# A graph layer on one core: completion signals of TensorE in the second gather stage, from drains to the matmuls themselves

## The chip, the cores and the metric

The kernel runs on one core of a Trainium2 chip. The metric is the device time of one execution in microseconds, the median over several runs. A core has five engines that run side by side and wait for one another by semaphores: TensorE (PE; its weight loads are listed as PEld), VectorE (DVE), ScalarE (ACT), GpSimd (POOL) and SyncE (SP). GpSimd, SyncE and ScalarE also issue DMA transfers here.

## The reference

The input is a graph with 6,250 nodes of 128 features and 100,000 edges, sorted by their destination. Two layers follow one another, each with a residual and a layer norm:

1. a relational layer: the messages `x[src] * norm` are summed by destination and edge type, multiplied by one matrix for each type (a mixture of 8 basis matrices), and a self-loop, a bias and a ReLU follow;
2. an edge layer: for every edge `e = (x[dst] - x[src]) @ theta.T + x[src] @ phi.T`, a batch norm over all edges, a ReLU, a product with `fc1`, a second batch norm and ReLU; the result is averaged over the edges of each destination, and a ReLU follows.

The stage of this document computes the first `e` of the second layer, for all edges. `theta` and `phi` act on nodes, so the kernel has two node tables in DRAM: `btab` (what an edge takes from its source) and `atab` (what it takes from its destination; as three bf16 parts that add up to the f32 value). An edge's `e` is a row of one plus a row of the other. The stage also counts the edges of every node, and the statistics of the batch norm.

## The kernel before, in words

Edges are handled in tiles of 128, chunks of 4 tiles (512 edges) and groups of 4 chunks. There are 49 groups and 196 chunks, the last one partly filled (782 tiles hold edges). The first gather stage (L682, to about 1250 us) belongs to the relational layer, the second one, the edge stage (about 1350 to 2515 us), to the edge layer. After it come a pass over the stored `e` (to 2700 us), the pass that sums by destination (to 3050 us) and the nodes.

In the edge stage each engine has its own program, written out by hand, with loops over pairs of groups. For every chunk:

- **GpSimd** takes one `g_free` and issues four indirect DMAs (L697), one a tile: each brings the 128 rows of `btab` that the sources name into a tile of `G`. `G` has room for two groups, so eight chunks.
- **SyncE** takes one `aw_free` and loads the 80 rows of `atab` from the chunk's least destination on (L618) into one of four buffers `aw`. Once a group it loads the digits of the destinations (L599).
- **TensorE** (`edge_features`) waits for the gathers and for a free bank of PSUM (`e_free`, four banks), and turns the four tiles into the bank (L906, f32). It waits for `aw` and for `ohT_ready`, and adds the destination's row by three matmuls against a one-hot matrix (L911, the "lookup"). It waits for `cnt_oh` and adds four small products to the node counts in bank 7 (L918). Then it spreads the digits of the chunk after next over all partitions (`spread_dst`, L895), into bank 0 or 1. At the end stands a drain (L938), which ends when TensorE has nothing left in work, and which increments `look_done`; `cnt_done` (L939) and `d_ready` (L941) are incremented by the sequencer after it.
- **VectorE** is one chunk ahead: it takes `d_ready` and compares the spread digits with the row numbers, which gives `ohT` (L1477); it takes `cnt_done` and makes the two one-hot factors of the counts (L1466, L1467, two buffers); it takes `e_copied` of an earlier chunk and measures its moments (L1504).
- **ScalarE** takes `look_done`, increments `g_free` (L1099) and `aw_free` (L1100), copies the bank to SBUF (L1101), and increments `e_free` and `e_copied`. Once a group it stores 1 MB of `e` to DRAM (L1107).

All waits go through the helper `take` (L56), so L56 stands in the rows wherever an engine waited for a semaphore. Chunks whose destinations reach beyond 80 nodes would need further windows; there is a second copy of the loop for them (`wide_chunks`), which these inputs don't use: all 196 drains of the trace are those of L938.

In the first gather stage the same four gathers a chunk (L682) fill `G`. TensorE multiplies each tile (L780), and the last of a chunk's four products increments the semaphore that ScalarE's copy (L1046) waits for; the copy's sequencer also gives `g_free` (L1042). A second product (L791) follows from the copy. There is no drain on TensorE in that stage. An f32 product stands as two matmuls in the trace.

Of the kernel before, what the change touches and what calls it, by code (L numbers as in the profile page):

```python
# [52 lines left out]
def take(eng, sem, n=1):  # L53

    eng.wait_ge(sem, n)
    eng.sem_inc(sem, -n)  # L56
# [17 lines left out]
def gnn_kernel(nc, x, src, dst, etype, norm, weight, w_comp, loop_w, h_bias,  # L74
# [38 lines left out]
    def sem(name):  # L113
        return ctx.enter_context(nc.semaphore(name))

    with ctx:  # L116
# [193 lines left out]
        cnt_done = sem("cnt_done")  # L310
# [26 lines left out]
        d_ready = sem("d_ready")  # L337
        ohT_ready = sem("ohT_ready")
        look_done = sem("look_done")
        look_first = sem("look_first")  # L340
# [37 lines left out]
        def reached(eng, name, s, value):  # L378

            eng.wait_ge(s, value)  # L380
            eng.sem_inc(ticks[name], 1)

        def by_pairs(eng, n, body, head=1, tail=0):

            for i in range(2 * head):
                body(i, i % 2, i // 2)
            with eng.Fori(head, n // 2 - tail) as i:
                body(2 * i, 0, i)
                body(2 * i + 1, 1, i)
            for i in range(n - 1 - 2 * tail, n):  # L390
                body(i, i % 2, i // 2)
# [32 lines left out]
        def gathered(g, k, use):  # L424

            return 16 * (TPC * use + len(real_tiles(g, k)))
# [38 lines left out]
        def last(i, n):  # L465
            return isinstance(i, int) and i == n - 1

        def after(g, h, use, k):

            if k + 1 < CPG:  # L470
                return g, h, use, k + 1
            if last(g, NG):
                return None
            return g + 1, 1 - h, use + h, 0

        def widest_chunk(eng):

            return eng.value_load(widest_c[0:1, 0:1], min_val=0, max_val=NXW)

        def reach_of(eng, c):  # L480

            return eng.value_load(bounds[0:1, bass.ds(c, 1)], min_val=SPAN, max_val=SPAN * (NXW + 1) - 1)
# [17 lines left out]
        def by_width(eng, w, loop):  # L500

            with eng.If(w >= 1):
                loop(True)
            with eng.If(w < 1):
                loop(False)
# [12 lines left out]
        def further_windows(eng, reach, body):  # L518

            with eng.If(reach >= 2 * SPAN):  # L520
                with eng.Fori(1, reach // SPAN) as i:
                    body(i)
# [203 lines left out]
        def _(pe):  # L726
# [24 lines left out]
            for k, a in enumerate((theta_s, phi_s, fc1_s)):  # L751
                mm = pe.transpose(PS[:, 6, k * D:(k + 1) * D], a[:, :], ident[:, :])
# [139 lines left out]
            def spread_dst(g, h, use, k):  # L892
                if k == 0:
                    reached(pe, "pe", dig_in[h], 16 * (use + 1))
                pe.matmul(PS[:, k % 2, :], onesb[0:2, :], digits[:, h, k * CHUNK:(k + 1) * CHUNK],  # L895
                          start=True, stop=True)

            def edge_features(wide_chunks):
                def one(g, h, use):
                    for k in range(CPG):  # L900
                        if wide_chunks:
                            reach = reach_of(pe, CPG * g + k)
                        reached(pe, "pe", b_gathered[CPG * h + k], gathered(g, k, use))
                        take(pe, e_free)
                        for q in range(TPC):
                            pe.matmul(PS[:, 2 + k, q * TILE:(q + 1) * TILE], G[:, h, TPC * k + q, :], ident[:, :],  # L906
                                      start=(q == 0), stop=False, is_transpose=True, skip_group_check=True)
                        reached(pe, "pe", aw_in[k], 16 * (g + 1))
                        take(pe, ohT_ready)
                        for a in range(3):  # L910
                            mm = pe.matmul(PS[:, 2 + k, :], aw[0:WIN, k, a, :], ohT[0:WIN, k % 2, :],  # L911
                                           start=False, stop=(a == 2), skip_group_check=True)
                        if wide_chunks:
                            mm.then_inc(look_first, 1)

                        take(pe, cnt_oh)
                        for q in range(TPC):
                            mm = pe.matmul(PS[:, 7, 0:NW], oh_lo[:, k % 2, q, :], oh_hi[:, k % 2, q, :],  # L918
                                           start=(isinstance(g, int) and g == 0 and k == 0 and q == 0),
                                           stop=(last(g, NG) and k == CPG - 1 and q == TPC - 1), skip_group_check=True)  # L920

                        def further(i):
                            take(pe, awx_in, 16)
                            take(pe, ohTx_ready)
                            for a in range(3):
                                mm = pe.matmul(PS[:, 2 + k, :], awx[0:WIN, a, :], ohTx[0:WIN, :],
                                               start=False, stop=(a == 2), skip_group_check=True)
                            mm.then_inc(lookx_done, 1)
                        if wide_chunks:
                            further_windows(pe, reach, further)  # L930
                        nxt = after(g, h, use, k)
                        nxt = nxt and after(*nxt)
                        if nxt:
                            spread_dst(*nxt)
                        if wide_chunks:
                            pe.drain().then_inc(cnt_done, 1)
                        else:
                            pe.drain().then_inc(look_done, 1)  # L938
                            pe.sem_inc(cnt_done, 1)  # L939
                        if nxt:  # L940
                            pe.sem_inc(d_ready, 1)  # L941
                by_pairs(pe, NG, one)
            pe.wait_ge(widest_c_known, 1)
            for k in range(2):
                spread_dst(0, 0, 0, k)
            pe.drain().then_inc(d_ready, 2)
            by_width(pe, widest_chunk(pe), edge_features)


# [772 lines left out]
```

## Time and profile before

| | |
|---|---|
| time, median of 3 runs | 3090.55 us (3073.56 to 3092.17) |
| the profiled execution | 3090.62 us, span 3088.8 us |
| TensorE (PE) busy | 1948.1 us (63%) |
| VectorE (DVE) busy | 1365.8 us (44%) |
| ScalarE (ACT) busy | 614.7 us (20%) |
| GpSimd (POOL) busy | 1605.7 us (52%) |
| mean granted clock of TensorE | 0.712 |

The span is from the first to the last instruction of one profiled execution. Busy time counts an engine's own work, not its waits. The ends of matmuls are modelled, their starts are not. An entry such as `[2.61 <-POOLq L56]` says that the engine was idle for 2.61 us before the instruction, and that a wait at L56 on its own queue ended that time; `issue` stands where the profile shows nothing that was waited for, or only the engine's own pace.

### The profile page before, as it was taken

Reading aid. Unit: us, or ns where it says so; the run is one execution under the profiler, and the core shown is the slowest. Engines: PE = TensorE matmul, PEld = TensorE weight load, DVE = VectorE, ACT = ScalarE, POOL = GpSimd, SP = SyncE. Lnnn points to the kernel's source line nnn. Section 1 sums busy time; section 2 is a strip of 40 time slices with the busy share of each in tenths; the row PEclk is TensorE's granted clock in tenths of the full one; section 3 lists DMA queues with packets and bytes.
Section 4 is the critical chain, followed back from the end, with each engine's and each line's share of the span. In section 5 each row is a group of like instructions: output and inputs, shape, how many; then the busy total and the mean of one; then the engine's idle time right before and its main releaser. Section 6 shows DMA issues by size and latency. Waiting matters only on the chain. (4 is left out here: it accounts for less than half of the span.)

```text
span 3088.8 us, 42986 instructions
## 1 busy us (share of the span) xinstructions
PE 1948.1 (63%) x10210; PEld 1494.5 (48%) x10211; DVE 1365.8 (44%) x3584; ACT 614.7 (20%) x1004; POOL 1605.7 (52%) x1759
## 2 busy tenths in 40 slices
PE   2666566656666666635554545445555579999997
PEld 2555465645655556622222222222222234499996
DVE  4333333333433333533333333333333358877776
ACT  2111111111111111411010101010101137534434
POOL 5665665666666664246666666666666620092002
PEclk9778777778778787855555555555555569999999
DMA  3221212121222211223333333333333349534443
GB/s 87 54 55 53 59 51 56 52 60 54 59 59 53 59 54 40 90 86 95 103 99 94 96 95 93 95 108 96 95 94 96 108 178 308 185 121 143 145 149 96
DMA packets 124080, 291.20 MB, mean 94 GB/s; under 512 B 34957, under 2 KB 77506, under 8 KB 106224
## 3 DMA queue, kind: packets, MB, share of 16 engines
q1 hardware_dynamic: 65856, 136.12, 13.5%
q0 software_dynamic: 50048, 102.50, 12.8%
q10 hardware_dynamic: 8112, 51.91, 4.3%
q14 instruction: 47, 0.39, 0.0%
q8 instruction: 17, 0.28, 0.0%
HBM read 227.22 MB, written 63.18 MB: 94 GB/s over the span
## 5 line engine op out<-in xcount | busy, mean ns | idle before, releaser
L697 POOL DMA_INDIRECT G<-btab,srcT x782 | 737.5, 943 | 534.9 <-POOLq L56 278.6
L682 POOL DMA_INDIRECT G<-in_x,srcT x782 | 746.3, 954 | 469.1 <-issue 233.3
L906 PE MATMUL PS<-ident,G 128*128 128x128 f32 x784 | 212.9, 427 | 568.9 <-PEq L56 335.9
L906 PEld LDWEIGHTS PS<-ident,G 128*128 128x128 f32 x784 | 140.1, 217 | 662.5 <-issue 662.5
L791 PE MATMUL PS<-BIG 128*128 128x192 f32 (+1 forms) x1584 | 352.0, 372 | 126.4 <-issue 124.6
L780 PE MATMUL PS<-BIG,G 128*128 128x192 f32 x1564 | 362.9, 393 | 91.2 <-issue 57.6
L791 PEld LDWEIGHTS PS<-BIG 128*128 128x128 f32 x1584 | 312.8, 222 | 152.9 <-issue 152.6
L1477 DVE TENSOR_SCALAR ohT<-PS,node_col 80x512 bf16<-80x512 f32 x196 | 146.2, 746 | 536.6 <-DVEq L56 317.2
L780 PEld LDWEIGHTS PS<-BIG,G 128*128 128x128 f32 x1564 | 328.6, 237 | 105.3 <-issue 104.8
L1046 ACT ACTIVATE BIG<-PS 128x768 f32<-128x768 f32 x196 | 156.3, 809 | 1032.7 <-ACTq L56 887.4
L1313 DVE SCALAR_TENSOR_TENSOR BIG<-PS,dst0T,BIG 128x192 f32<-128x192 f32 x784 | 324.2, 416 | 79.9 <-issue 67.1
L1322 DVE TENSOR_TENSOR ACC<-ACC,PS 128x24 f32 x782 | 135.3, 173 | 447.3 <-DVEq L56 324.1
L1101 ACT ACTIVATE BIG<-PS 128x512 f32<-128x512 f32 x196 | 117.0, 597 | 1057.0 <-ACTq L56 1029.4
L911 PE MATMUL PS<-ohT,BIG 80*128 80x512 bf16 x588 | 291.4, 633 | 1.9 <-PEq L56 1.9
L978 PE MATMUL PS<-fc1sT,G 128*128 128x128 f32 x1568 | 216.3, 282 | 2.9 <-DVEq L1598 1.5
L1504 DVE BATCH_NORM_STATS2 stats<-BIG 128x6 f32<-128x512 f32 x192 | 131.2, 684 | 181.4 <-issue 112.2
L992 PE MATMUL PS<-BIG 128*128 128x80 f32 x1568 | 198.9, 270 | 0.0
L978 PEld LDWEIGHTS PS<-fc1sT,G 128*128 128x128 f32 x1568 | 192.3, 193 | 3.4 <-DVEq L1598 1.8
L992 PEld LDWEIGHTS PS<-BIG 128*128 128x128 f32 x1568 | 190.6, 192 | 0.0
L1145 ACT ACTIVATE G<-BIG,small 128x512 f32<-128x512 f32 x188 | 137.8, 803 | 207.9 <-ACTq L56 207.9
L958 PE MATMUL PS<-G,fc1T 128*128 128x512 f32 x392 | 170.1, 597 | 6.2 <-PEq L56 6.2
L722 POOL TENSOR_SCALAR X<-X,ln_st,ln_r 128x128 f32<-128x128 f32 x20 | 15.7, 795 | 262.9 <-DVEq L1682 262.9
(182 smaller groups left out, 1834.3 us busy)
## 6 DMA issues: line engine op xcount, KB each, us to landing
BIG<-spill SPq DMA_DIRECT2D x90, 1024.0 KB, 4.9
spill<-BIG ACTq DMA_DIRECT2D x49, 1024.0 KB
G<-in_x,srcT POOLq DMA_INDIRECT x782
G<-btab,srcT POOLq DMA_INDIRECT x782
typ_i<-in_edge_type SPq DMA_DIRECT2D x97, 128.0 KB
BIG<-atab SPq DMA_DIRECT2D x196, 60.0 KB
atab<-BIG SPq DMA_DIRECT2D x12, 384.0 KB
xn<-in_x SPq DMA_DIRECT2D x48, 64.0 KB
```

The lines of the kernel that those rows point to most:

```text
L682: nc.gpsimd.indirect_dma_start(out=G[0:n, g % 2, t, :], out_offset=None, in_=x, in_offset=bass.IndirectOffsetOnAxis(ap=srcT[0:n, TPG * g + ...
L697: nc.gpsimd.indirect_dma_start(out=G[0:n, g % 2, t, :], out_offset=None, in_=btab[:, :], in_offset=bass.IndirectOffsetOnAxis(ap=srcT[0:n, ...
L780: mm = pe.matmul(PS[:, 2 * c + q // 2, (q % 2) * ZW:(q % 2 + 1) * ZW], G[:, h, TPC * k + q, :], soh[:, p, TPC * c + q, :, :].rearrange("p ...
L791: mm = pe.matmul(PS[:, bank, tiles.start * TWIN:tiles.stop * TWIN], basis[:, b, :], zs[:, p, tiles, b, :], start=(b == 0), stop=(b == B - ...
L906: pe.matmul(PS[:, 2 + k, q * TILE:(q + 1) * TILE], G[:, h, TPC * k + q, :], ident[:, :], start=(q == 0), stop=False, is_transpose=True, sk ...
L911: mm = pe.matmul(PS[:, 2 + k, :], aw[0:WIN, k, a, :], ohT[0:WIN, k % 2, :], start=False, stop=(a == 2), skip_group_check=True)
L958: pe.matmul(PS[:, CPG * h + k, :], fc1T[:, :], hot[:, h, k * CHUNK:(k + 1) * CHUNK], start=True, stop=True).then_inc(e2_ready, 1)
L978: mm = pe.matmul(PS[:, k, q * D:(q + 1) * D], hot[:, h, t * TILE:(t + 1) * TILE], fc1sT[:, :], start=True, stop=True)
L992: mm = pe.matmul(PS[:, 4 + k, 0:WIN], R2[:, k, q, :], oh3[:, k, q, :], start=(q == 0), stop=(q == TPC - 1))
L1046: act.activation(zs[:, p, TPC * c:TPC * c + 2 * banks, :, :].rearrange("p (a q) k n -> p a (q k n)", a=banks), PS[:, 2 * c:2 * c + banks, ...
L1313: ins = dve.scalar_tensor_tensor(out=soh[:, p, j, :, :], in0=over(steps0, B, TWIN), scalar=dst0T[:, bass.ds(t, 1)], in1=each(coefs[:, bass ...
L1477: dve.tensor_scalar(ohT[0:WIN, k % 2, :], PS[0:WIN, k % 2, :], node_col[0:WIN, 0:1], None, ALU.is_equal).then_inc(ohT_ready, 1)
```

## The change

In the edge stage TensorE's drains are taken out, and three matmuls signal in their place: the last lookup of a chunk increments `look_done` (the copy of the loop for wide chunks already had a signal there, `look_first`), the last count product increments `cnt_done`, and each spread of digits increments `d_ready`. The same goes for the two spreads and the drain ahead of the loop. The number of increments of each semaphore stays.

```diff
@@ spread_dst
                 pe.matmul(PS[:, k % 2, :], onesb[0:2, :], digits[:, h, k * CHUNK:(k + 1) * CHUNK],
-                          start=True, stop=True)
+                          start=True, stop=True).then_inc(d_ready, 1)
@@ edge_features
                         for a in range(3):
                             mm = pe.matmul(PS[:, 2 + k, :], aw[0:WIN, k, a, :], ohT[0:WIN, k % 2, :],
                                            start=False, stop=(a == 2), skip_group_check=True)
-                        if wide_chunks:
-                            mm.then_inc(look_first, 1)
+                        mm.then_inc(look_first if wide_chunks else look_done, 1)
 
                         take(pe, cnt_oh)
                         for q in range(TPC):
                             mm = pe.matmul(PS[:, 7, 0:NW], oh_lo[:, k % 2, q, :], oh_hi[:, k % 2, q, :],
...
+                        mm.then_inc(cnt_done, 1)
...
                         if nxt:
                             spread_dst(*nxt)
-                        if wide_chunks:
-                            pe.drain().then_inc(cnt_done, 1)
-                        else:
-                            pe.drain().then_inc(look_done, 1)
-                            pe.sem_inc(cnt_done, 1)
-                        if nxt:
-                            pe.sem_inc(d_ready, 1)
                 by_pairs(pe, NG, one)
             pe.wait_ge(widest_c_known, 1)
             for k in range(2):
                 spread_dst(0, 0, 0, k)
-            pe.drain().then_inc(d_ready, 2)
             by_width(pe, widest_chunk(pe), edge_features)
```

## Rows read from the trace of the kernel before

**Rows 1.** Busy times of the edge stage: stretch, engines, PEclk, DMA share, GB/s

```profile
1350.00:2515.00 1165.00, 598.86 (x2344) 319.29 (x2345) 445.40 (x827) 116.43 (x195) 712.97 (x751) 0.50 0.31 96
```

**Rows 2.** Groups of instructions, 1400 to 2490 us: busy us, mean ns, idle before

```profile
L906 PE MATMUL PS<-ident,G 128*128 128x128 f32 x720 | 195.6, 427 | 539.4 <-PEq L56 313.4 <-issue 226.0
L1477 DVE TENSOR_SCALAR ohT<-PS,node_col 80x512 bf16<-80x512 f32 x180 | 134.3, 746 | 508.8 <-DVEq L56 297.8 <-issue 206.9 <-PEq L941 4.1
L1466 DVE TENSOR_TENSOR oh_lo<-PS,loT 128x512 bf16<-128x512 f32 x179 | 121.1, 677 | 0.0
L1467 DVE TENSOR_TENSOR oh_hi<-PS,hiT 128x196 bf16<-128x196 f32 x179 | 62.3, 348 | 0.0
L1504 DVE BATCH_NORM_STATS2 stats<-BIG 128x6 f32<-128x512 f32 x180 | 123.1, 684 | 168.4 <-issue 110.0 <-DVEq L56 58.4
```

**Rows 3.** GpSimd's gathers, 1400 to 2490 us: durations; waits (total us, times, longest)

```profile
L697 POOL DMA_INDIRECT G<-btab,srcT x720: 867/944/955, 1400.2 to 2489.7; - x180
POOL G L697 <- POOLq L56: 172.7, 54, 4.0
POOL G L697 <- ACTq L1099: 26.6, 18, 2.0
```

**Rows 4.** The drain's line: duration ns min/median/max, first and last start

```profile
L938 PEldq DRAIN  x196: 1965/3914/10583, 1353.6 to 2514.6; - x196
```

**Rows 5.** Timeline of TensorE in the edge stage: start us, us, instruction [idle before]

```profile
2005.91 1.09 PE L906 MATMUL PS<-ident,G 128*128 128x128 f32 x4 [4.12 <-PEq L56]
...
2008.38 0.60 PE L895 MATMUL PS<-BIG,onesb 2*128 2x512 bf16 x1
2009.66 1.09 PE L906 MATMUL PS<-ident,G 128*128 128x128 f32 x4 [0.68 <-issue]
2010.54 1.49 PE L911 MATMUL PS<-ohT,BIG 80*128 80x512 bf16 x3
...
2012.13 0.60 PE L895 MATMUL PS<-BIG,onesb 2*128 2x512 bf16 x1
2018.34 1.08 PE L906 MATMUL PS<-ident,G 128*128 128x128 f32 x4 [5.61 <-PEq L56]
```

**Rows 6.** Timeline of ScalarE in the same stretch

```profile
2009.26 0.60 ACT L1101 ACTIVATE BIG<-PS 128x512 f32<-128x512 f32 x1 [3.15 <-ACTq L56]
2017.94 0.60 ACT L1101 ACTIVATE BIG<-PS 128x512 f32<-128x512 f32 x1 [8.09 <-ACTq L56]
```

**Rows 7.** Timeline of GpSimd in the same stretch

```profile
2006.17 0.94 POOL L697 DMA_INDIRECT G<-btab,srcT  x1 [2.50 <-POOLq L56]
...
2015.05 0.94 POOL L697 DMA_INDIRECT G<-btab,srcT  x1 [0.30 <-issue]
2018.60 0.94 POOL L697 DMA_INDIRECT G<-btab,srcT  x1 [2.61 <-POOLq L56]
```

**Rows 8.** GpSimd's gathers in the first stage, 60 to 1250 us, as rows 3

```profile
L682 POOL DMA_INDIRECT G<-in_x,srcT x750: 875/944/1470, 68.7 to 1217.3; - x188
POOL G L682 <- ACTq L1042: 127.9, 41, 4.2
POOL G L682 <- POOLq L56: 98.7, 45, 15.4
```

**Rows 9.** Timeline of TensorE and ScalarE in the first gather stage

```profile
703.74 2.77 PE L780 MATMUL PS<-BIG,G 128*128 128x192 f32 x16
708.85 0.32 PE L791 MATMUL PS<-BIG 128*128 128x192 f32 x1 [2.34 <-issue]
...
713.50 1.51 ACT L1046 ACTIVATE BIG<-PS 128x768 f32<-128x768 f32 x2 [11.35 <-ACTq L56]
```

**Rows 10.** Timeline of TensorE after the last gather

```profile
2507.27 1.09 PE L906 MATMUL PS<-ident,G 128*128 128x128 f32 x4 [0.68 <-PEq L56]
...
2511.03 1.09 PE L906 MATMUL PS<-ident,G 128*128 128x128 f32 x4 [0.68 <-PEq L56]
```

## The prediction

> **What bounds the kernel now.** I began with the page and its chain of waits. The chain holds only the last few instructions, so it says nothing of the stage that is changed; I went to that stage by its lines. The edge stage runs from about 1350 to 2515 us. The busy times of that stretch [rows 1] show no engine full: GpSimd 713 of 1165 us, TensorE 599, at a granted clock of 0.50 (the 1.2 GHz level).
>
> What could bound it is read from the groups. GpSimd issues four gathers a chunk, 943 ns each with a usual gap of 0.30 us between them [rows 3, 7], so a chunk costs it 4 * 1.25 = 5.0 us. VectorE's four large instructions a chunk add up to 0.746 + 0.677 + 0.348 + 0.684 = 2.46 us [rows 2]. TensorE's chunk lasts 3.07 us from the first transpose (2009.66) to the end of the spread (2012.13 + 0.60) [rows 5]. So GpSimd should set the pace, yet the 180 chunks between 1400 and 2490 us took 1090 / 180 = 6.06 us each.
>
> The waits tell why. In that stretch GpSimd stood 172.7 + 26.6 = 199.3 us in 72 waits for a free chunk of G [rows 3]. Without the wait each would have been the usual 0.30 us gap, so the waits cost 199.3 - 72 * 0.30 = **178 us**, 2.47 us apiece, one in every 180 / 72 = 2.5 chunks. This is the ceiling of what the change can give in the stage. The free chunk is signalled by ScalarE (L1099) once it has look_done, and look_done comes from TensorE's drain.
>
> The drain's own row [rows 4] has a median of 3.9 us and a longest of 10.6 us. It starts while matmuls are still queued, so its length alone isn't the loss; the timeline [rows 5, 6] is. The chunk from 2005.91 ends with a spread at 2008.38 + 0.60 = 2008.98, and ScalarE starts 0.28 us later. The next chunk's spread ends at 2012.73, but ScalarE starts at 2017.94, 5.2 us later, and TensorE's next transpose at 2018.34, after 5.61 us idle. Nothing that the profile names was running on TensorE. In that time GpSimd had issued its eighth gather (2015.05, ended 2015.99), then waited 2.61 us for the chunk that this very drain had to free [rows 7]. So the picture of a cycle is: GpSimd resumes (2006.17), TensorE's first chunk passes at once (+2.8 us), the second, which ends at +6.6 us, is held until gathers have stopped, GpSimd runs dry, the signal comes, and it begins again: two chunks in 12.43 us.
>
> **Is it the drain, or TensorE's signals as such?** The first gather stage has the same gathers and no drain. There a run of L780 starts at 703.74 and lasts 2.77 us: two chunk products of equal length, so the first one's own signal (it stands on its last matmul) was due near 705.1 (an estimate, half of the run). ScalarE's copy that waits for it starts at 713.50, after 11.35 us idle, and TensorE itself issues L791 singly, with 2.34 us idle before the first one [rows 9]. So while gathers flow, a matmul's own signal is held as well, and so is the issue of further matmuls. This is the main evidence against the change.
>
> A page speaks to the same point: the Trainium skill, Perfetto Trace Analysis, section "Tensor Engine Instruction (MATMUL, LD_WEIGHTS)", says that the end shown for a matmul is an estimate and that its semaphore goes out only when PSUM has acknowledged the write. By that rule the matmuls would end late, not the drain, and the change would give almost nothing; the trace of the first stage agrees in the 8.4 us between 705.1 and 713.50.
>
> **The change part by part.** *Removed:* 196 drains, 196 increments of cnt_done and 194 of d_ready on TensorE's sequencer. Where nothing holds the drain, a chunk step has 0.68 us between the last matmul and the next transpose [rows 5, 10]; inside a chunk TensorE's groups follow without idle time. Without the drain this gap goes, hidden under GpSimd's 5.0 us a chunk, except after the last gather (2489.7 [rows 3]): the seven chunks that then remain run at 2511.03 - 2507.27 = 3.76 us each, and become 3.07. That is 7 * 0.68 = 5 us, on the path to the end of the stage. If VectorE became the bound there (2.46 us of work), nothing changes.
>
> *Added:* three signals a chunk on matmuls that are there already. No row has their price alone. From below: the runs of L780 with two signals inside them show no gap [rows 9], so 0. From above: the 0.68 us gap of the three sequencer steps that they replace. I take 0, the nearer row. Even the upper end would lie under TensorE's idle time, 539.4 / 180 = 3.0 us a chunk [rows 2]; with that cover gone it would be 0.68 * 196 = 133 us, which the range doesn't hold, since the gap goes with the steps.
>
> A second rule of the skill speaks against the change: TensorE: Matmul & The Clock Gate, section "The cost: per-tile semaphore tail", gives 26.3 ns for each matmul that signals, one after another. By it the sum would be worse by an estimated 3 * 26.3 ns * 196 = 15 us if they stood on the path; no run here shows it.
>
> *Moved:* look_done goes from behind the spread to the last lookup, 0.70 us earlier in the chunk (2010.54 + 1.49 = 2012.03 against 2012.73). The lost gap brings the second chunk forward by another 0.68 us, so its look_done falls at +5.2 us after GpSimd resumes instead of +6.6. ScalarE then gives g_free, aw_free and its copy earlier. SP's window loads and the digits are four chunks and a group ahead, and SP and ScalarE's queues issue the same DMAs in the same order; nobody waits for them. cnt_done and d_ready stay in order on VectorE: it takes d_ready of the chunk after next first, and it is one chunk ahead.
>
> *What is late next:* the drain also kept TensorE from the following chunk. Its transposes need a free bank (four deep), its lookups an ohT that VectorE made from the spread two chunks back. So when chunk B's signals are held, TensorE can still do all of chunk C; chunk D's lookups need B's spread signal. At the next quiet moment B and C are signalled together, if B was not signalled in time already.
>
> **The sum.** A cycle today frees on the strict pattern one held chunk and one that passes (2), and 2.5 on average. After the change it frees one or two held ones and two that pass (3 to 4). I take 3.5. Waits: 180 / 3.5 = 51 instead of 72, at 2.47 us: 127 us instead of 178, a gain of 51, and 5 at the tail: 56 us. At 3 chunks: 60 waits, 148 us, gain 35; at 4: 45 waits, 111 us, gain 72. The profiled execution took 3090.62 us (span 3088.8 and 1.8 around it), the median is 3090.55, so the sum holds for both: 3090.6 - 56 = **3035 us**, 3019 to 3056 for this case alone. It stays in the sum that the waits keep their length.
>
> **The rivals.**
> *No change (chance 0.27).* The signals on matmuls are held just as long and only the tail is won: 3085 us. For it: the first stage [rows 9], whose 86 waits cost 226.6 - 86 * 0.30 = 201 us in 187.5 chunks [rows 8], 1.07 us a chunk against 0.99 here, without any drain. If the edge stage took over exactly that price it would be 196 * 0.08 = 16 us worse, 3101 with the tail. Against it: in the held chunk all matmuls still started without a gap, so what is held is what comes last, and look_done no longer comes last.
> *GpSimd becomes the bound (0.08).* All 178 us and the tail go: 2908 us. TensorE's 3.07 us and VectorE's 2.46 would allow it; against it speaks that the hold is seen in both gather stages whenever several gathers are in flight. A higher granted clock in a denser stage would push this way.
> *Slower (0.10).* TensorE, not stopped any more, sends a third chunk into the gather flow; its instructions wait singly as L791's do, and the signals of the held chunks stand behind them. The number of waits stays at 72, but each lasts longer. The first stage's waits for ScalarE have a mean of 127.9 / 41 = 3.1 us, the longest here is 4.0 [rows 3, 8]. At 3.5 us: 72 * 3.2 = 230 us, 52 worse, less 5: 3138 us; at 4.0 us 3174. It decides from a wait of 3.3 us on (72 * 3.0 = 216, +38 - 5).
> *That the change doesn't do what it says* can be left out as a case of its own: the plain branch is the one that runs, with 196 drains in it [rows 4].
>
> **The numbers.** Forecast 0.55, no change 0.27, GpSimd's bound 0.08, slower 0.10. Faster by over 1% means below 3060 us; a measurement of this kernel can hardly tell less than 1% from no change. Faster: nearly all of 0.55, and 0.08, less what the forecast may fall short: 0.58. Slower by over 1% (above 3121): 0.10. The same: 0.32. The range leaves out GpSimd's bound and the slower case: from 2985 (six chunks a cycle: 30 waits, 74 us, gain 104 and the tail 5, gives 2982) to 3100 (the first stage's price).
>
> **What would show it.** Right: no drain in the edge stage, the step of the last seven chunks near 3.1 us, ScalarE's copy starting within 0.3 us of the second chunk's lookups after a resume, and GpSimd's waits near 50 with a mean under 3 us. Wrong: about 70 waits again, with copies 5 us behind their lookups (no change); waits above 3.3 us with single matmuls among long gaps in the edge stage (slower); gathers 1.25 us apart throughout (GpSimd's bound).

## The result, and the profile after

The changed kernel took 3044.34 us (median of 4 runs, 3042.78 to 3047.93), the kernel before 3091.36 us beside it: a ratio of **0.987** (95% interval 0.984 to 0.990). The forecast was 3035 us, range 2985 to 3100. The time is right, but one term of the sum is not.

Line numbers shift by up to eight: L1469 was L1477, L1093 was L1101 (the copy), L917 was L918; there is no drain. The profiled execution took 3043.06 us, against 3090.62. Three moments of either trace split the 47.6 us; two of them, the first and the last gather, stand in these rows (before, then after):

```profile
L697 POOL DMA_INDIRECT G<-btab,srcT x782: 867/944/958, 1288.1 to 2489.7; - x196
L697 POOL DMA_INDIRECT G<-btab,srcT x782: 869/944/961, 1278.9 to 2448.5; - x196
```

| part of the profiled execution | before | after | difference |
|---|---|---|---|
| start to the first gather of the edge stage | 1288.1 | 1278.9 | -9.2 |
| first to last gather (start to start) | 1201.6 | 1169.6 | -32.0 |
| last gather to the end of ScalarE's last copy | 27.8 | 20.7 | -7.1 |
| from there to the end | 573.1 | 573.9 | +0.8 |

The first line isn't the change's: nothing before the edge stage was edited, and over the twelve kernels below that moment lies anywhere from 1275.7 to 1296.7 us. What the change gave is in the second and third lines, 39 us in these two executions; the interval of the ratio puts it between 30 and 48 us.

The busy times of the stage after, to be set beside [rows 1]:

```profile
1350.00:2470.00 1120.00, 604.28 (x2315) 290.03 (x2315) 431.35 (x819) 115.84 (x194) 708.90 (x747) 0.50 0.32 100
```

GpSimd fills 709 of 1120 us, still not full; the granted clock is 0.50 as before. Its gathers and waits from 1400 us on, and the groups, answering to [rows 2, 3]:

```profile
L697 POOL DMA_INDIRECT G<-btab,srcT x712: 869/944/961, 1399.3 to 2448.5; - x178
POOL G L697 <- issue: 202.6, 651, 1.7
POOL G L697 <- POOLq L56: 176.3, 61, 4.3
```

```profile
L911 PE MATMUL PS<-ohT,BIG 80*128 80x512 bf16 x534 | 257.8, 620 | 486.5 <-issue 168.7 <-DVE ohT L1469 138.3 <-PEq L56 131.1
L906 PE MATMUL PS<-ident,G 128*128 128x128 f32 x716 | 199.5, 434 | 0.0
L1469 DVE TENSOR_SCALAR ohT<-PS,node_col 80x512 bf16<-80x512 f32 x178 | 132.2, 743 | 614.5 <-DVEq L56 382.4 <-remote 190.0 <-issue 40.7
L1093 ACT ACTIVATE BIG<-PS 128x512 f32<-128x512 f32 x178 | 106.3, 597 | 939.2 <-ACTq L56 846.3 <-issue 54.1 <-DVEq L1521 38.8
```

The lookups before, from 1400 to 2490 us, had no idle time ahead of them:

```profile
L911 PE MATMUL PS<-ohT,BIG 80*128 80x512 bf16 x540 | 267.6, 633 | 0.0
```

TensorE's idle time has moved from the transposes (539.4 us ahead of L906 before, 0.0 now) to the lookups (486.5 us ahead of L911): it now runs on into the next chunk and stands at the next `ohT`, whose spread is not signalled yet. The lists put some stops of GpSimd under "issue" and some 0.3 us gaps under a wait, so from here on a **stop** is a distance of over 1.5 us between the starts of two gathers, where 1.25 is usual, and its cost is what exceeds 1.25. From 1400 us to the last gather there were 82 stops of 2.34 us (191.6 us) before, and 48 of 3.37 us (161.8 us) after. One cycle after, as a timeline:

```profile
1781.27 0.60 ACT L1093 ACTIVATE BIG<-PS 128x512 f32<-128x512 f32 x1 [15.66 <-ACTq L56]
1781.93 0.94 POOL L697 DMA_INDIRECT G<-btab,srcT  x1 [3.85 <-POOLq L56]
...
1782.34 0.60 ACT L1093 ACTIVATE BIG<-PS 128x512 f32<-128x512 f32 x1 [0.47 <-ACTq L56]
...
1784.21 0.60 ACT L1093 ACTIVATE BIG<-PS 128x512 f32<-128x512 f32 x1 [1.28 <-DVEq L1521]
...
1784.22 1.11 PE L906 MATMUL PS<-ident,G 128*128 128x128 f32 x4
...
1785.19 1.44 PE L911 MATMUL PS<-ohT,BIG 80*128 80x512 bf16 x3
...
1786.89 0.60 ACT L1093 ACTIVATE BIG<-PS 128x512 f32<-128x512 f32 x1 [2.08 <-ACTq L56]
...
1787.54 18.07 SPq L618 DMA_DIRECT2D BIG<-atab  x4
...
1789.29 1.44 PE L911 MATMUL PS<-ohT,BIG 80*128 80x512 bf16 x3 [0.91 <-DMA BIG<-atab]
...
1795.01 1.44 PE L911 MATMUL PS<-ohT,BIG 80*128 80x512 bf16 x3 [2.54 <-DVE ohT L1469]
...
1800.66 0.94 POOL L697 DMA_INDIRECT G<-btab,srcT  x1 [0.31 <-issue]
...
1804.75 0.60 ACT L1093 ACTIVATE BIG<-PS 128x512 f32<-128x512 f32 x1 [17.27 <-ACTq L56]
...
1805.42 0.94 POOL L697 DMA_INDIRECT G<-btab,srcT  x1 [3.81 <-POOLq L56]
1805.64 1.44 PE L911 MATMUL PS<-ohT,BIG 80*128 80x512 bf16 x3 [7.44 <-PEq L56]
1805.82 0.60 ACT L1093 ACTIVATE BIG<-PS 128x512 f32<-128x512 f32 x1 [0.47 <-ACTq L56]
```

Four copies a cycle: two held chunks come out together (0.47 us apart), and two more pass. GpSimd then issues 16 gathers (1781.93 to 1800.66) and stops for 3.81 us beyond its last gather, where [rows 7] show 2.61 us after eight. The lookups that start at 1789.29 and 1795.01 have their copies only at 1804.75 and 1805.82: the first signal is 14.0 us late, where the one of [rows 6] was 5.2. It is the signal that is late and not ScalarE: the trace records no change of the semaphore `look_done` between 1786.64 and 1804.51 us, and ScalarE's wait ends at 1804.53. The tail, answering to [rows 10]:

```profile
2454.50 1.11 PE L906 MATMUL PS<-ident,G 128*128 128x128 f32 x4
...
2457.53 1.11 PE L906 MATMUL PS<-ident,G 128*128 128x128 f32 x4
...
2460.55 1.11 PE L906 MATMUL PS<-ident,G 128*128 128x128 f32 x4
```

After the last gather a chunk takes 3.03 us instead of 3.76.

### The profile page after: what moved, and what is told of

Read it like the earlier page. It is cut to its first block and busy times, and to the rows that moved or that the text cites. A ratio compares the mean times of both kernels' runs of the same rounds, so it can differ in the third digit from the quotient of the medians.

```text
span 3041.2 us, 42399 instructions
## 1 busy us (share of the span) xinstructions
PE 1975.9 (65%) x10210; PEld 1477.7 (49%) x10211; DVE 1357.8 (45%) x3584; ACT 614.1 (20%) x1004; POOL 1606.5 (53%) x1759
## 5 line engine op out<-in xcount | busy, mean ns | idle before, releaser
L911 PE MATMUL PS<-ohT,BIG 80*128 80x512 bf16 x588 | 284.3, 621 | 516.9 <-issue 168.7
L791 PE MATMUL PS<-BIG 128*128 128x192 f32 (+1 forms) x1584 | 369.6, 382 | 142.5 <-issue 140.6
L1469 DVE TENSOR_SCALAR ohT<-PS,node_col 80x512 bf16<-80x512 f32 x196 | 145.5, 742 | 649.6 <-DVEq L56 413.1
L791 PEld LDWEIGHTS PS<-BIG 128*128 128x128 f32 x1584 | 323.9, 229 | 180.7 <-issue 180.4
L911 PEld LDWEIGHTS PS<-ohT,BIG 80*128 80x128 bf16 x588 | 64.0, 127 | 626.4 <-issue 623.2
L1093 ACT ACTIVATE BIG<-PS 128x512 f32<-128x512 f32 x196 | 117.0, 597 | 1019.7 <-ACTq L56 915.3
L906 PE MATMUL PS<-ident,G 128*128 128x128 f32 x784 | 218.4, 434 | 4.2 <-PEq L56 4.2
L984 PEld LDWEIGHTS PS<-BIG 128*128 128x128 f32 x1568 | 190.6, 192 | 0.0
L906 PEld LDWEIGHTS PS<-ident,G 128*128 128x128 f32 x784 | 140.0, 216 | 89.8 <-issue 89.8
```

Of the source, the lines that this page charges most:

```text
L791: mm = pe.matmul(PS[:, bank, tiles.start * TWIN:tiles.stop * TWIN], basis[:, b, :], zs[:, p, tiles, b, :], start=(b == 0), stop=(b == B - ...
L984: mm = pe.matmul(PS[:, 4 + k, 0:WIN], R2[:, k, q, :], oh3[:, k, q, :], start=(q == 0), stop=(q == TPC - 1))
L1469: dve.tensor_scalar(ohT[0:WIN, k % 2, :], PS[0:WIN, k % 2, :], node_col[0:WIN, 0:1], None, ALU.is_equal).then_inc(ohT_ready, 1)
```

## The experiments

All twelve in one table: the ratio of times to the kernel before, first to last gather, the one long stop before the first copy (start to start), and the stops from 1400 us on.

| kernel | ratio [95%] | first to last gather | first stop | stops | their cost | mean | cost per gather |
|---|---|---|---|---|---|---|---|
| before | 1 | 1201.6 | 29.7 | 82 | 191.6 | 2.34 | 0.27 |
| after | 0.987 [0.984, 0.990] | 1169.6 | 27.1 | 48 | 161.8 | 3.37 | 0.23 |
| e1 bare drain | 1.003 [1.001, 1.005] | 1199.3 | 28.1 | 66 | 191.1 | 2.90 | 0.27 |
| e2 look_done last | 0.992 [0.990, 0.994] | 1175.8 | 28.8 | 54 | 166.8 | 3.09 | 0.23 |
| e3 g_free early | 0.987 [0.983, 0.990] | 1160.2 | 23.7 | 53 | 154.2 | 2.91 | 0.22 |
| e4 light TensorE | 0.985 [0.982, 0.988] | 1154.0 | 26.1 | 43 | 151.5 | 3.52 | 0.21 |
| e5 small windows | 0.989 [0.987, 0.991] | 1180.5 | 28.9 | 51 | 171.2 | 3.36 | 0.24 |
| e6 small stores | 0.988 [0.986, 0.991] | 1177.7 | 29.3 | 45 | 166.2 | 3.69 | 0.23 |
| e7 all small | 0.983 [0.982, 0.985] | 1170.8 | 28.1 | 48 | 160.5 | 3.34 | 0.23 |
| e8 four ahead | 0.986 [0.984, 0.988] | 1179.4 | 28.5 | 46 | 168.0 | 3.65 | 0.23 |
| e9 half the rows | 0.987 [0.983, 0.992] | 1172.4 | 30.0 | 57 | 193.4 | 3.39 | 0.27 |
| e10 half the bytes | 0.989 [0.985, 0.993] | 1167.5 | 27.9 | 47 | 162.2 | 3.45 | 0.23 |
| e11 long pause | 1.013 [1.007, 1.018] | 1259.5 | none | 187 | 259.4 | 1.39 | 0.36 |
| e12 short pause | **0.974** [0.971, 0.978] | 1137.4 | none | 185 | 146.5 | 0.79 | 0.21 |

(e9's gathers are shorter, 0.91 us, so its stops count against 1.21 us. In e11 and e12 each pause counts as a stop.)

**e1: a drain that signals nothing.** At the end of each chunk, with the matmuls' own signals kept:

```diff
                         if nxt:
                             spread_dst(*nxt)
+                        pe.drain()
```

> The changed kernel with the drain back at the end of each chunk, but without a signal: look_done, cnt_done and d_ready stay on the matmuls. Theory A (while gathers flow, everything that TensorE finishes is held back in order, and a wait of GpSimd ends when gathers have stopped and TensorE's backlog is worked off): TensorE can't run a chunk ahead in the hold, so a wait frees one held chunk and two that pass, 3 instead of 4, and each wait is short again, about 2.5 us over the usual gap as in the kernel before instead of about 3.5: some 62 waits, 155 us, 3035 to 3060 us in all. Theory B (the drain itself is what costs, a matmul's own signal is not held): the drains' time comes back, 3085 to 3095 us. Theory C (the place of the signal is all that counts): as the changed kernel, 3044 us, with its 4 chunks a wait.

The whole gain went: 3086.73 us against 3079.7 beside it. The drain's row and GpSimd's waits in that kernel:

```profile
L935 PEldq DRAIN  x196: 1992/4194/14632, 1346.8 to 2505.7; - x196
```

```profile
POOL G L697 <- issue: 208.1, 648, 2.8
POOL G L697 <- POOLq L56: 200.7, 66, 7.0
```

So it is the drain as a barrier for TensorE, more than the place of the signals, that cost the time. The signals themselves are seldom late there: 124 of the 196 copies start within 0.3 us of their lookups, against 53 in the changed kernel. What waits again are the transposes, 513.2 us of idle time ahead of L906 from 1400 to 2440 us. The time is theory B's; theory A had the number of stops (62 forecast) and missed the time. The stops did become fewer (82 to 66; over the whole stage 50 of 68 follow 12 gathers), while their cost stayed at 191 us, in part by four stops of 6.6 to 6.7 us that the changed kernel doesn't have and that stay unexplained. Fewer stops need not be less stopping: the first sign of what the prediction missed.

**e2: the old place of look_done, no drain.** A one-column matmul behind the spread gives look_done instead of the last lookup (it writes into the bank of the counts, which are left out so):

```diff
-                        mm.then_inc(look_first if wide_chunks else look_done, 1)
+                        if wide_chunks:
+                            mm.then_inc(look_first, 1)
...
+                        if not wide_chunks:
+                            pe.matmul(PS[:, 7, 256:257], onesb[0:2, :], onesb[0:2, 0:1],
+                                      start=True, stop=True, skip_group_check=True).then_inc(look_done, 1)
```

> The changed kernel, no drains, but look_done is signalled last in the chunk: by one more matmul of one column behind the spread (the wide copy is unchanged). Theory A: the second chunk after GpSimd resumes ends its spread about 0.7 us later than its lookups and is held more often; about 3 chunks a wait at the long 3.5 us, 3065 to 3095 us. Theory B: no drain, so 3040 to 3050 us. Theory C: the place is lost, 3085 to 3095 us.

3055.77 us, between the expectations. The cost of the stops rose by 5 us to 166.8, first to last gather by 6 us; by the ratios (0.992 against 0.987) some 15 us were lost. Together with e1: the larger part of the gain is the barrier's, the smaller one the place's.

**e3: g_free from TensorE.** The last transpose of a chunk frees it, without the way over ScalarE:

```diff
-                            pe.matmul(PS[:, 2 + k, q * TILE:(q + 1) * TILE], G[:, h, TPC * k + q, :], ident[:, :],
+                            mm = pe.matmul(PS[:, 2 + k, q * TILE:(q + 1) * TILE], G[:, h, TPC * k + q, :], ident[:, :],
...
+                        mm.then_inc(g_free, 1)
...
-                    act.sem_inc(g_free, 1)
```

> The changed kernel with g_free given by the last transpose of a chunk, on TensorE, instead of by ScalarE after look_done: G is read by the transposes alone. Theory A: the signal falls 1.5 us and ScalarE's 0.25 us earlier in the chunk, and TensorE transposes one chunk further ahead than it looks up; 5 chunks a wait at 3.5 us, 39 waits, about 135 us, 3010 to 3030 us. Theories B and C: the signal is already early, 3035 to 3045 us.

3037.03 us, no measurable step from the changed kernel (the intervals nearly coincide) and within what theories B and C gave; theory A's 3010 to 3030 us and 39 stops didn't come, though the signal now comes from the end of the transposes (1784.22 + 1.11 in the cycle above) instead of the end of the lookups (1785.19 + 1.44), 1.3 us earlier in a chunk. Earlier signals alone don't shorten the stops much.

**e4: less work on TensorE.** One lookup part instead of three and one count product instead of four (the others are left out):

```diff
-                        for a in range(3):
-                            mm = pe.matmul(PS[:, 2 + k, :], aw[0:WIN, k, a, :], ohT[0:WIN, k % 2, :],
-                                           start=False, stop=(a == 2), skip_group_check=True)
+                        mm = pe.matmul(PS[:, 2 + k, :], aw[0:WIN, k, 0, :], ohT[0:WIN, k % 2, :],
+                                       start=False, stop=True, skip_group_check=True)
...
```

> The changed kernel with less work for TensorE in the edge stage: one lookup part instead of three and one count product instead of four, so 7 instead of 12 matmuls a chunk; the tables' lower parts and three quarters of the counts are left out. Theory A: there is less in the backlog, so the waits of GpSimd are shorter (2.5 to 3 us over the usual gap instead of 3.5) or rarer; 2960 to 3010 us. Rival: the hold is set by the gathers alone, whatever TensorE has done meanwhile: the same waits, 4 chunks apart and 3.5 us long, 3030 to 3045 us.

3034.92 us. In the stretch from 1350 to 2430 us TensorE is busy 408 us instead of 578, but the gathers took 1154.0 us against 1169.6. Half of the stops (21 of 44 over the stage) now follow 20 gathers, five chunks, and those cost 3.75 us each. TensorE's work sets how many chunks pass in a cycle, and changes little in what stopping costs in all (151.5 us against 161.8). The rival had the time right and the distance of the stops wrong; theory A's time, 2960 to 3010 us, didn't come.

After these four the lengths could be sorted by the number of gathers since the stop before. In this kernel and the changed one: 2.66 us after 12 gathers (7 stops), 3.34 and 3.55 after 16 (17 and 37), 3.75 after 20 (21). That gave **theory G**: every gather leaves some 0.2 us of something behind it that is worked off only when GpSimd stands still.

These means mix in stops that were cut short. Behind such a one the next stop comes after only 4 gathers, and the two together cost what one stop costs after all the gathers: 0.78 + 2.83 = 3.61 us after 12 and 4 gathers in the changed kernel, and eight such pairs in e9 (below) cost 4.11 to 4.17 us, where one stop after 16 gathers has a median of 4.11. So something is indeed carried over. Without these pairs the medians are 2.97 us after 12 gathers, 3.54 after 16 and 3.94 after 19 in the changed kernel, and 3.51 after 16 and 4.11 after 20 in e4. That is no fixed 0.2 us a gather: a straight line through them (an estimate) has some 1.2 us for each stop, and 0.14 to 0.15 us for each gather. The 0.2 us is what both come to in runs of about 16 gathers.

**e5, e6, e7: the other traffic.** In e5 a chunk's window of `atab` has 16 rows instead of 80, in e6 the stores of `e`, and the loads that read it back later, have 16 partitions instead of 128, and e7 has both, and e4's edit:

```diff
-                        sp.dma_start(aw[0:WIN, k, :, :].rearrange("p a d -> p (a d)"), atab[bass.ds(base, WIN), :]).then_inc(aw_in[k], 16)
+                        sp.dma_start(aw[0:16, k, :, :].rearrange("p a d -> p (a d)"), atab[bass.ds(base, 16), :]).then_inc(aw_in[k], 16)
...
-                act.dma_start(spill[bass.ds(g, 1), :, :].rearrange("o p n -> (o p) n"), stage[:, stage_of(g, h), :]).then_inc(stored[h], 16)
+                act.dma_start(spill[bass.ds(g, 1), 0:16, :].rearrange("o p n -> (o p) n"), stage[0:16, stage_of(g, h), :]).then_inc(stored[h], 16)
```

> The changed kernel, with 16 rows of a chunk's window of atab loaded instead of 80 and lookups over 16 rows (this leaves out most of the destination's part of e). Instructions and signals stay where they are; the windows' packets on the DMA queues fall to a fifth. Theory G (the backlog that a wait of GpSimd works off is made by the gathers themselves, about 0.2 us a gather): waits stay as in the changed kernel, about 50 in the edge stage with a mean of 3.3 us, first to last gather 1160 to 1175 us, time 3030 to 3045 us. Rival W (the backlog is made by the window loads' packets, which share the DMA engines with the gathers): waits fall below 1.5 us each, first to last gather below 1110 us, time below 2990 us.

> The changed kernel, with 16 of 128 partitions of e stored once a group and read back by the later passes (this leaves out most of e there). The later passes lose DMA work as well, so the verdict is taken from the edge stage alone. Theory G (backlog from the gathers): first to last gather 1155 to 1175 us, about 50 waits with a mean of 3.3 us, the time shorter only by what the later passes gain. Rival S (backlog from the 1 MB stores): one wait in four at most is shortened per store, first to last gather below 1120 us.

> The changed kernel with the windows of 16 rows, the stores of 16 partitions, and one lookup part and one count product a chunk on TensorE instead of three and four (this leaves out most of the destination's part, of the counts and of the stored e): the gathers almost alone. Verdict from the edge stage. Theory G: what is left still stops every 16 to 20 gathers for over 3 us; first to last gather 1140 to 1170 us. Rival (other traffic and TensorE's work together make the backlog): waits below 1 us, first to last gather near the issue rate, 782 x 1.25 = 977 us, at any rate below 1050.

Little moved: 0.24, 0.23 and 0.23 us a gather. e5 ended 5.5 us over the first-to-last time that theory G gave it and 18 us over its total, e6 2.7 us and e7 0.8 us over their first-to-last times; the kernel before took 3095.89 us beside them, more than in the other series, and e5's ratio is near the changed kernel's. The busy times from 1350 to 2430 us of e7, with the columns of [rows 1]:

```profile
1350.00:2430.00 1080.00, 421.87 (x1282) 185.85 (x1281) 412.67 (x778) 109.89 (x184) 692.95 (x733) 0.50 0.22 53
```

53 GB/s instead of 100 and 422 us of TensorE instead of 578, and GpSimd gets just as little further: 692.95 us busy, 691.06 in the changed kernel. The rivals (window loads, stores, all of it together) fall.

**e8: four chunks ahead instead of eight.**

```diff
+            take(pool, g_free, CPG)
             for g in range(NG):
...
```

> The changed kernel, with GpSimd allowed four chunks of G ahead instead of eight. Theory G with the ring as the only stop (a hold lasts until GpSimd has used up its free chunks and the backlog of its gathers is worked off): runs of at most 8 gathers, twice as many waits (about 95) of 1.6 to 2.0 us each, by the lengths that followed runs of 8 gathers before; 95 x 1.8 = 171 us, so first to last gather again 1160 to 1185 us and the time 3035 to 3060 us. Rival H (a hold has a length of its own, some 3.3 us whatever came before it): 95 x 3.3 = 314 us, first to last gather about 1300 us, time above 3150 us.

Neither premise came true: half the credits don't halve the runs. 44 of 49 stops still follow 16 gathers, at 3.69 us:

```profile
POOL G L698 <- issue: 199.4, 654, 0.3
POOL G L698 <- POOLq L56: 174.6, 47, 4.2
POOL G L698 <- ACTq L1093: 4.3, 1, 4.3
```

A run is as long as the chunks that come free at a resume, two held and two that pass; the other four chunks of G gave no longer runs here. The time is 3053.83 us, as theory G put it, though not for its reason. So no run sets the length of a run by itself.

**e9, e10: smaller gathers.** 64 of 128 rows a gather, and then 128 rows of 256 bytes:

```diff
-                        n = rows_of(TPG * g + t)
+                        n = min(64, rows_of(TPG * g + t))
```

```diff
-                            out=G[0:n, g % 2, t, :], out_offset=None, in_=btab[:, :],
+                            out=G[0:n, g % 2, t, 0:64], out_offset=None, in_=btab.rearrange("r (h d) -> (r h) d", h=2),
```

> The changed kernel, with 64 of a tile's 128 rows gathered in the edge stage (the other half of each tile of G keeps older numbers, so half of e is left out). As many gather instructions as before, half the rows and bytes. Theory R (what a wait of GpSimd works off grows by some 0.2 us with each gather because of its rows or bytes): waits after 16 gathers fall from 3.5 to about 1.7 us; first to last gather below 1080 us; time about 2950 us. Rival I (it grows with the number of gather instructions, whatever they bring): waits after 16 gathers stay at 3.3 to 3.7 us, first to last gather 1150 to 1180 us. Rival H (a hold has its own length, set by TensorE's side): waits and span as in the changed kernel too.

> The changed kernel, with each gather bringing 128 rows of 256 bytes instead of 512 (the table is read as rows of half the length, so other numbers come than the reference's). As many gather instructions and rows as before, half the bytes. If the waits grow with the bytes: about 1.7 us after 16 gathers and first to last gather below 1080 us. If they grow with the rows or with the instructions: 3.3 to 3.7 us after 16 gathers and 1150 to 1180 us. Together with the run on half the rows this tells rows from bytes.

Theory R, which was G with rows or bytes as its cause, is refuted: 4.16 us after 16 gathers in e9 (27 stops), 3.56 in e10 (42). Rival I had e9's first-to-last time right (1150 to 1180 us), but its stops are longer than the 3.3 to 3.7 us that it gave. The gathers of e9:

```profile
L697 POOL DMA_INDIRECT G<-btab,srcT x782: 873/908/923, 1296.7 to 2469.1; - x196
```

Half the rows make an instruction 0.04 us shorter, and the stage no shorter at all. What has to be worked off doesn't shrink with what the gathers bring. That it grows along a run, rather than being a fixed length, rests on the lengths inside each kernel (e7, without the pairs: a median of 3.65 us after 16 gathers, 4.26 after 20, one stop of 4.91 after 24). Whether it grows with the number of gathers or with the time that they take isn't told apart.

**e11: a pause behind each chunk's gathers.**

```diff
+        idle = sb("idle", [P, 800])
...
                         ).then_inc(b_gathered[CPG * (g % 2) + k], 16)
+                    nc.gpsimd.memset(idle[:, :], 0.0).then_inc(shift_ready, 1)
+                    take(pool, shift_ready)
```

> The changed kernel, with GpSimd clearing a scratch tile of 800 columns after each chunk's gathers in the edge stage: an estimated 0.7 us by its memset of 6656 columns in 5.7 us, and some 0.1 us to wait for it, so about 0.8 us a chunk without a gather in flight being issued, 196 x 0.8 = 157 us in all. Theory R (the waits work off a backlog of 0.2 us a gather, which the pause would work off as well): waits shrink by about 0.8 us a chunk, from 3.5 us after 16 gathers to 1 us or less, and first to last gather stays within 20 us of the 1170 us of the changed kernel. Rival H (signals come through only when GpSimd has run dry, and then after some 3.3 us): the pauses come on top, first to last gather 1300 us or more, time above 3150 us. Third (signals pass in each pause): no waits are left at all, first to last gather 977 + 157 = 1134 us.

The third case came true in kind, at 1259.5 us from first to last gather instead of 1134, with a longer pause than estimated: 0.78 us of clearing and 0.60 beyond the usual gap until the next gather, 1.38 us a chunk. GpSimd, TensorE and ScalarE in that kernel (L909 is L906, L914 is L911, L1096 is L1093):

```profile
1803.30 0.94 POOL L698 DMA_INDIRECT G<-btab,srcT  x1 [0.30 <-issue]
...
1804.24 0.78 POOL L702 MEMSET idle<- 128x800 f32 x1
...
1805.92 0.95 POOL L698 DMA_INDIRECT G<-btab,srcT  x1 [0.90 <-POOLq L56]
...
1806.14 1.09 PE L909 MATMUL PS<-ident,G 128*128 128x128 f32 x4 [3.37 <-PEq L56]
...
1807.02 1.49 PE L914 MATMUL PS<-ohT,BIG 80*128 80x512 bf16 x3
...
1808.76 0.60 ACT L1096 ACTIVATE BIG<-PS 128x512 f32<-128x512 f32 x1 [5.84 <-issue]
```

The lookups end at 1807.02 + 1.49 = 1808.51 by the model, and the copy starts 0.25 us later, in the middle of flowing gathers. All 196 copies of that run start 0.257 to 0.263 us behind their lookups. In the changed kernel the median is 2.79 us, the longest 18.9. Chunks are hardly waited for any more (192 of 203 stops are the bare pause); the pauses cost more than the stops they replace (259.4 against 161.8 us), and the kernel is slower than before.

**e12: the pause cut short.** 16 columns instead of 800:

```diff
-                    nc.gpsimd.memset(idle[:, :], 0.0).then_inc(shift_ready, 1)
+                    nc.gpsimd.memset(idle[:, 0:16], 0.0).then_inc(shift_ready, 1)
```

> The changed kernel with the pause of the run before cut short: GpSimd clears 16 columns instead of 800 after each chunk's gathers, an estimated 0.01 to 0.06 us, and then needs the 0.6 us that it took from the end of the longer clearing to the next gather above its usual gap. A chunk then takes 5.0 + 0.65 = 5.65 us where no wait is added, against 6.38 us with the long pause (6.38 x 196 = 1250 us) and 1170 / 196 = 5.97 us in the changed kernel. If a pause of any length lets the signals pass (all copies of ScalarE 0.26 us behind their lookups, as with the long pause): no waits for a chunk, first to last gather 1107 to 1125 us, time near 2985 us. Theory R (a backlog of 0.2 us a gather, 0.8 us a chunk, of which the pause works off 0.65): copies on time for some chunks, then a short wait of about 0.6 us every four chunks or so; first to last gather 1130 to 1160 us, time 3005 to 3035 us. Rival H (below some length a pause lets nothing through): runs of 16 gathers with waits above 3 us on top of the pauses, first to last gather above 1270 us, time above 3140 us.

3007.61 us, **2.6% under the kernel before** and the best here; first to last gather 1137.4 us, within what theory R gave (the expectations of e11 and e12 call the backlog so, whatever makes it). A pause is 0.72 us a chunk:

```profile
1807.32 0.12 POOL L702 MEMSET idle<- 128x16 f32 x1
1808.35 0.96 POOL L698 DMA_INDIRECT G<-btab,srcT  x1 [0.90 <-issue]
```

179 of its 203 stops over the stage are such a pause alone, and the 23 longer than 2.15 us from start to start exceed it by 14 us together. The copies are late again (half by over 6.2 us), but GpSimd seldom runs out of chunks. A pause of 0.72 / 4 = 0.18 us a gather leaves signals late, one of 1.38 / 4 = 0.35 us doesn't; where between them the change lies isn't measured. Most of the gain over the changed kernel comes from elsewhere than the steady part, which fell from 161.8 to 146.5 us. Up to 1400 us stops and pauses cost 14.6 us instead of 33.0, since the first stop fell away, and the tail behind the last gather took 12.4 us instead of 20.7. The start of the stage in the changed kernel, where TensorE still builds a table (L883) while the first eight chunks are gathered:

```profile
1306.88 2.04 PE L883 MATMUL PS<-ctab,ACC 128*128 128x128 f32 x8 [11.96 <-issue]
1324.38 3.75 PE L883 MATMUL PS<-ctab,ACC 128*128 128x128 f32 x16 [15.46 <-PEq L56]
...
1344.70 0.94 POOL L697 DMA_INDIRECT G<-btab,srcT  x1 [26.14 <-POOLq L56]
```

And with the short pause (L886 is that table):

```profile
1303.83 3.75 PE L886 MATMUL PS<-ctab,ACC 128*128 128x128 f32 x16 [3.22 <-issue]
1310.40 2.05 PE L886 MATMUL PS<-ctab,ACC 128*128 128x128 f32 x8 [2.81 <-issue]
...
1343.19 0.95 POOL L698 DMA_INDIRECT G<-btab,srcT  x1 [2.22 <-ACTq L1094]
```

In the changed kernel TensorE's table stood for 12 and 15 us at a time while gathers flowed, and GpSimd then waited 26 us for the first chunk to come free. With pauses the table is done earlier, and the wait is 2.2 us.

## Why the prediction was right, and which step was not

*The bound.* Right: GpSimd stops for chunks of G, and they come late because TensorE's signals, or TensorE itself at its drain, are held while gathers flow. e11 shows the hold by its absence, e1 the drain's share.

*Removed drains, the tail.* Right in kind and nearly in size: 5 us forecast from 7 * 0.68, 7.1 measured. The step fell to 3.03 us (3.07 forecast), which gives 7 * 0.73 = 5.1; the rest is that seven copies start after the last gather instead of eight.

*Added signals.* Right at nothing: transposes start with no idle time ahead of them (0.0 us), and the step of the tail, with the signals in it, is 3.03 us, no longer than the 3.07 forecast without a price for them. The Trainium skill's tail of 26.3 ns for each (TensorE: Matmul & The Clock Gate, section "The cost: per-tile semaphore tail") had no place to show in a stage with that much idle time on TensorE. In the last chunks, where TensorE has none, the 3.03 us show nothing of it either.

*Chunks a cycle.* 3.5 forecast, at most 4; measured 4 in 37 of 51 stops over the stage. 51 stops from 1400 us on were forecast, 48 came. The picture "two held, two that pass" is the timeline above, and the second chunk's copy came 0.26 us behind its lookups (1786.63 to 1786.89).

*The length of a stop.* This is the term that was mis-sized. The text said "It stays in the sum that the waits keep their length", 2.47 us; they became 3.37. 48 * 3.37 = 162 us instead of 51 * 2.47 = 127, and the gain from the stops was 30 us instead of 51. Its sign of being right, a mean under 3 us, failed with it. The prediction took each stop as a toll to be paid once a cycle. Only some 1.2 us of a stop is that (the estimate behind e4); the rest grows with the gathers since the last stop. So 24 stops fewer (72 to 48, without the second halves of stops cut short) gave 30 us, 1.24 us each and not 2.47, and the last column of the table stays at 0.21 to 0.24 us in every kernel without drains or long pauses, but for e9. The rival for slower had this half right: it priced stops of over 3.3 us, but with their number unchanged.

*The time.* That its 3035 us came so near to the 3044 us was in part luck: 30 + 7 and 2 or 3 us of the first stop would have made 3052, and in the profiled execution the other 9 us fell ahead of the edge stage, which the change doesn't touch.

*The first stage as evidence.* It was read rightly (matmuls' own signals are held too), and the prediction gave it too little weight as a reason why the ceiling of 178 us could not be won by the place of signals. The Trainium skill, Perfetto Trace Analysis, section "Tensor Engine Instruction (MATMUL, LD_WEIGHTS)", says that a matmul's semaphore goes out when PSUM has acknowledged the write. No run here shows PSUM's side, but in e11 ScalarE's copies of the same writes start 0.26 us behind their modelled end, so nothing in the matmuls themselves makes the signals late.

*Open.* What the gathers leave behind isn't seen in any row. The data isn't it: in the cycle above the last gather's packets end at 1802.98 us, the copy is let go 1.5 us later, and halving rows or bytes shortens no stop. That the held signals themselves, or the time, are what adds up and not the gathers isn't excluded: no run has fewer signals a chunk on TensorE. The 0.27 us a gather in the kernel before fits its shorter runs, mostly of 8 and 12 gathers, which pay the part of each stop that doesn't grow more often; e1's 0.27 has its four long stops in it; e9's 0.27 is unexplained.

## What to carry to other kernels

Before pricing stops by their number, sort their lengths by what happened since the stop before: where length grows with the run, rarer stops are longer stops, and an avoided stop is worth only the part that doesn't grow (an estimated 1.2 us of 3.5 here). A producer that holds up others while its requests flow can gain by a short pause of its own: 0.72 us a chunk took the place of 3.4 us stops here and let the start of the stage through. And a drain costs what it keeps the engine from doing next, which its own row doesn't show.

## What the runs showed that was not expected

- GpSimd takes 0.77 us from a wait that it has to stand at to its next gather (1805.15 to 1805.92 in e11, and the same median over the 50 longer waits of the changed kernel), which makes even a 0.12 us clearing a 0.72 us pause.
- While signals are held, SyncE's sequencer is held up as well: from 1786 to 1804 us more than half of its 20 instructions take some 0.7 us or more each in the trace, and four window loads (L618) stretch over 18.07 us in the cycle above. From 1400 to 2400 us 517 of 1566 take 0.6 to 0.8 us; in e11 it is 13 of 1442.
- A gather of half the rows takes 0.908 us instead of 0.944, and one of half the bytes 0.944: in these runs the instruction's length hardly depends on what it fetches.
